# Two of three duos of image 1 take one pair's denominator from scanned sums; the join of the images and the last duo are rearranged

## The chip, the core and the metric

The kernel runs on one core of one Trainium2 chip. Its engines run beside each other and meet by semaphores: TensorE (PE, its weight loads listed as PEld), VectorE (DVE), ScalarE (ACT), GpSimd (POOL), and SyncE (SP), which issues the DMAs. The metric is device microseconds of one execution, lower is better; a kernel's time is the median of its runs. One execution was taken with the hardware profiler, and it has a time and a span of its own.

## What is computed

The input is x, 2 x 128 x 128 x 192 (image, H, W, channel), float32, and the output is x plus a window ratio of the group-normalised x:

```python
def box_sum(x, axis, w): ...        # zero-padded sliding sum of width w
g = _gn(x)                          # 32 groups of 6 channels, mean and variance over H, W and the group
s     = box_sum(g, 2, 5)            # 5 wide along W
num   = box_sum(s * s, 3, 20)       # 20 wide along the channels
d     = box_sum(box_sum(g * g, 2, 5), 3, 20)
denum = d * norm                    # norm: how many columns of W the window really covers
return x + nan_to_num(num / denum, nan=1.0)
```

Mean and variance of an image are needed before any of its centred work can start.

## The kernel before

W lies on the 128 partitions. Four rows of H (768 columns of H and channel) are a duo, made of two pairs of 384 columns; an image has 32 duos, and n runs from 0 to 63 over both images. The load of image 1 and its statistics run beside the duos of image 0. PSUM holds four tiles, S, U, D and N, each of two banks, one bank for a pair; the duo's 384 columns leave 128 columns of each bank spare.

For one duo n of image 1 (and the last ones of image 0) the steps are:

- POOL subtracts the mean, `centre(n)` (line 358, tile xc).
- ACT squares it, `square_xc` (line 422). PE sums both along W with 5-wide bands: `box_u` gives U from the squares, `box_s` gives S from xc (line 520, 128 x 128 blocks).
- ACT copies U to SBUF, `keep_u` (line 436), and squares S, `square_s` (line 446).
- PE sums along the channels with 20-wide bands, scaled by the inverse variance (line 529): `sum_d` gives D, `sum_n` gives N.
- ACT takes the reciprocal root of D and squares it, which gives q (lines 473 and 479).
- DVE runs `quotient(n)`: t1 from D and q (line 776), t2 from N and q (line 779), ratio from both (line 785). A Newton step for the reciprocal is folded into these.
- POOL adds the ratio to x, `finish(n)` (line 364), and SP stores two duos at a time (line 288).

A duo is **summed** if its second pair does not go through `box_u` and `sum_d`. For that pair POOL scales xc to a padded line, `normalise` (line 376), ACT squares the line into the spare half of U, `square_line` (line 428), DVE makes 20-wide sums of it with two scans and an addition, `sum_windows` (lines 746, 749 and 752, result `of_20`), and PE sums `of_20` along W with one wide matmul (line 572). Before, every second duo from 35 on is summed, 15 of them.

The order is written out by hand. On PE each duo n is `sum_d(n)`, `box_u(n+2)`, `sum_n(n)`, `box_s(n+2)`. `sum_d(n)` waits until DVE has read D of duo n-1 (`t1_ready`), `sum_n(n)` until the ratio of n-1 is done (`ratio_ready`), since D and N have one buffer. ACT runs root and square of n, `keep_u(n+2)`, `square_xc(n+3)`, `square_line(n+3)`, `square_s(n+2)`. DVE runs `sum_windows(n+2)` ahead of t1 of n, if n+2 is summed. POOL runs `centre(n+4)`, `normalise(n+4)`, `finish(n)`.

At the **join** of the images, in duo 29, DVE sums the last statistics of image 1 (line 832), PE averages them over the partitions (line 597), DVE copies the mean to SBUF (line 677, in `spread_late`, which also prepares the variance up to line 703), and POOL can centre duo 32, the first of image 1. In duo 30 the variance follows. The **last duo**, 63, ends with an addition on DVE (line 846) in place of POOL's, and a store of its own (line 308).

Of the kernel before, what the change touches and what calls it, by code (L numbers as in the profile page):

```python
# [6 lines left out]
ALU = mybir.AluOpType  # L7
# [4 lines left out]
GROUPS = 32  # L12
# [19 lines left out]
TOTAL = BATCH * DUOS  # L32

# [22 lines left out]
FIRST_SUMMED, SUMMED_EVERY = DUOS + 3, 2  # L56
# [33 lines left out]
def window_ratio_kernel(nc, x, out):  # L90
    ctx = ExitStack()
    with ctx:
# [45 lines left out]
        padded, restart = sums[:, 0:PADDED], sums[:, PADDED:PADDED + LINE]  # L138
        rising, of_20 = sums[:, 1024:1024 + PADDED], sums[:, 1536:1536 + PCOLS]
        scale_c = sums[:, 2048:2048 + PCOLS]  # L140
# [17 lines left out]
        mean_in_psum = sem("mean_in_psum")  # L158
        offsets_in_psum = sem("offsets_in_psum")
# [40 lines left out]
        def d_bank(n):  # L200

            return S if n < SWAPPED and n % 2 else D
# [17 lines left out]
        def summed(n):  # L220
            return FIRST_SUMMED <= n < TOTAL and (n - FIRST_SUMMED) % SUMMED_EVERY == 0

        def nth_summed(n):
            return (n - FIRST_SUMMED) // SUMMED_EVERY
# [47 lines left out]
        def _(sp):  # L272
# [31 lines left out]
            last = TOTAL - 1  # L304
            sp.wait_ge(out_ready, last)
            sp.dma_start(dram_rows(out, last - 1), x_rows(last - 1)).then_inc(stored[1], 16)
# [6 lines left out]
        def _(pool):  # L313
# [53 lines left out]
            def normalise(n):  # L367

                k = nth_summed(n)
                if k:  # L370
                    pool.wait_ge(squares_ready, k)
# [4 lines left out]
                nc.gpsimd.tensor_tensor(rows_of(padded[:, C_LO:PADDED]), pair,  # L376
# [3 lines left out]
            def clear_sums():  # L380

                pool.wait_ge(n_ready, RAW_DUOS)
                nc.gpsimd.memset(padded, 0.0).then_inc(pool_own, 1)
# [9 lines left out]
            for n in range(TOTAL - 1):  # L393
                m = n + CENTRE_AHEAD
                if m == DUOS:
                    for j in range(len(LATE_SETS)):
                        wait_loaded1(pool, j)
                    pool.wait_ge(mean_ready, 2)
                    clear_sums()
# [4 lines left out]
                finish(n)  # L404

        @block.scalar
        def _(act):
# [16 lines left out]
            def square_line(n):  # L424

                act.wait_ge(scaled_ready, nth_summed(n) + 1)
                act.wait_ge(us_ready, n)
                nc.scalar.activation(squares_ps, padded, ACT.Square).then_inc(squares_ready, 1)
# [84 lines left out]
        def _(pe):  # L513
# [37 lines left out]
            def box_u(n):  # L551
# [6 lines left out]
                if summed(n - 1):  # L558
# [302 lines left out]
```

## Time and profile before

| | us |
|---|---|
| median of 3 runs | 382.54 (382.38 to 382.55) |
| the profiled execution, its own time | 381.17 |
| its span | 379.5 |
| PE busy | 355.8 (94%) |
| PE weight loads busy | 349.5 (92%) |
| DVE busy | 298.4 (79%) |
| ACT busy | 273.1 (72%) |
| POOL busy | 249.5 (66%) |
| granted PE clock, mean share of full speed | 0.998 |

Busy shares are means over the whole span and say which engine is nearly full, not which wait ends last at a place; for that the timeline and the chain of waits are read stretch by stretch. Matmul ends are modelled and the matmuls of a block overlap, so a block's length is better read from the chain, where each piece begins as the former ends. A recorded DVE or ACT instruction can end some hundredths of a microsecond after the next one on its engine has started, so what an instruction costs its engine is read from start to start.

### The profile page before, as it was taken

What the parts mean: (1) busy time and instruction counts of PE and PEld (TensorE: products, weight loads), DVE (VectorE), ACT (ScalarE), POOL (GpSimd) and SP (SyncE); (2) the same over time, 40 slices, a digit from 0 to 9 for tenths busy, and PEclk for the clock granted to TensorE, in tenths of its full rate; (3) what the DMA queues carried; (4) which work ended last, traced back from release to release, by engine and by line L of the source; (5) the groups of instructions that cost most, each with busy time, mean ns of one, the idle gap of its engine ahead of it and who ended that gap; (6) DMA issues with size and microseconds to landing.
All of it is one profiled execution on the core that took longest, in us unless ns stands there. A gap on an engine that the chain in (4) does not pass through costs nothing.

```text
span 379.5 us, 7832 instructions
## 1 busy us (share of the span) xinstructions
PE 355.8 (94%) x2960; PEld 349.5 (92%) x2960; DVE 298.4 (79%) x609; ACT 273.1 (72%) x383; POOL 249.5 (66%) x168
## 2 busy tenths in 40 slices
PE   1999979999999999999869999999999999999982
PEld 1999969999999999999869999999999999999981
DVE  2999964766679999999957877777778877777774
ACT  1455559989999999987726777777777777777751
POOL 4000064887888888887158877788777787777631
PEclk9999999999999999999999999999999999999999
DMA  8999300588999973222202222211222222222214
GB/s 243 327 328 329 105 2 0 168 252 263 290 281 282 287 241 106 85 85 83 85 0 85 85 84 85 82 54 53 64 85 85 83 85 85 83 86 83 66 53 134
DMA packets 66486, 50.84 MB, mean 134 GB/s; under 512 B 912, under 2 KB 66448, under 8 KB 66448
## 3 DMA queue, kind: packets, MB, share of 16 engines
q1 hardware_dynamic: 66448, 50.34, 42.8%
q8 instruction: 24, 0.39, 0.4%
q14 instruction: 14, 0.11, 0.1%
HBM read 25.17 MB, written 25.17 MB: 133 GB/s over the span
## 4 chain that ended last, share of the span: by engine, by line
PE 71%; DVE 7%; ACT 5%; issue 2%; POOL 1%; DVEq 0%; POOLq 0%; ACTq 0%
PE N L529 21%; PE U L520 17%; PE D L529 14%; PE S L520 11%; PE S L529 4%; DVE late_triples L668 3%; PE D L572 3%; ACT xs L455 1%; DVE ratio L776 1%; DVE N L779 1%; ACT q L473 1%; ACT xc L422 1%; POOL xc L358 1%; ACT q L479 1%; DVE ratio L785 1%
## 5 line engine op out<-in xcount | busy, mean ns | idle before, releaser
L364 POOL TENSOR_TENSOR xs<-xs,ratio 128x768 f32<-128x768 f32 x63 | 114.6, 1820 | 63.4 <-DVE ratio L785 63.4
L358 POOL TENSOR_TENSOR xc<-xs,mean_c 128x768 f32<-128x768 f32 x64 | 116.9, 1829 | 44.8 <-DVE mean_c L677 44.8
L776 DVE SCALAR_TENSOR_TENSOR ratio<-D,q 128x768 f32<-128x768 f32 x51 | 48.6, 952 | 43.0 <-ACT q L479 43.0
L785 DVE SCALAR_TENSOR_TENSOR ratio<-ratio,N 128x768 f32<-128x768 f32 x64 | 61.1, 954 | 6.4
L779 DVE SCALAR_TENSOR_TENSOR N<-N,q 128x768 f32<-128x768 f32 x64 | 61.5, 960 | 4.9 <-PE N L529 3.1
L473 ACT ACTIVATE q<-D 128x768 f32<-128x768 f32 x51 | 41.4, 811 | 28.1 <-PE D L529 18.4
L479 ACT ACTIVATE q<-q 128x768 f32<-128x768 f32 x64 | 54.1, 846 | 2.0
L520 PE MATMUL S<-b,xc 128*128 128x128 f32 x432 | 54.0, 275 | 0.0
L529 PE MATMUL N<-b_r,xs 128*128 128x138 f32 (+2 forms) x384 | 52.4, 285 | 0.0
L529 PE MATMUL N<-b,xs 128*128 128x138 f32 (+2 forms) x384 | 51.7, 283 | 0.3 <-DVE ratio L785 0.3
L446 ACT ACTIVATE xs<-S 128x768 f32<-128x768 f32 x36 | 29.2, 812 | 31.5 <-PE S L520 31.5
L520 PEld LDWEIGHTS S<-b,xc 128*128 128x128 f32 x432 | 51.2, 191 | 0.0
L529 PEld LDWEIGHTS N<-b,xs 128*128 128x128 f32 x384 | 48.5, 190 | 1.0 <-issue 0.9
L529 PEld LDWEIGHTS N<-b_r,xs 128*128 128x128 f32 x384 | 48.4, 190 | 0.3
L520 PEld LDWEIGHTS U<-b5d,xs 128*128 128x128 f32 x342 | 42.2, 191 | 6.6 <-ACT xs L422 2.9
L520 PE MATMUL U<-b5d,xs 128*128 128x128 f32 x342 | 44.1, 275 | 2.7 <-ACT xs L422 2.7
L668 DVE BATCH_NORM_STATS2 ratio<-xs 128x6 f32<-128x96 f32 x256 | 41.0, 263 | 5.9 <-DMA xs<-x 5.9
L436 ACT ACTIVATE u<-U 128x768 f32<-128x768 f32 (+1 forms) x63 | 45.2, 718 | 0.0
L520 PE MATMUL U<-b5d,xc 128*128 128x128 f32 x336 | 42.3, 276 | 0.8 <-ACT xc L422 0.4
L529 PE MATMUL D<-b,u 128*128 128x137 f32 (+2 forms) x294 | 40.8, 283 | 1.3 <-DVE ratio L776 1.3
L520 PEld LDWEIGHTS U<-b5d,xc 128*128 128x128 f32 x336 | 39.8, 191 | 1.4 <-ACT xc L422 0.9
L529 PEld LDWEIGHTS D<-b,u 128*128 128x128 f32 x294 | 37.6, 190 | 1.4 <-issue 1.4
(89 smaller groups left out, 452.6 us busy)
## 6 DMA issues: line engine op xcount, KB each, us to landing
out<-xs SPq DMA_DIRECT2D x31, 768.0 KB, 3.8
xs<-x SPq DMA_DIRECT2D x8, 1536.0 KB, 14.8
xs<-x SPq DMA_DIRECT2D x16, 768.0 KB, 5.3
out<-xs SPq DMA_DIRECT2D x2, 384.0 KB, 2.6
```

Source lines behind the costliest of these rows:

```text
L358: nc.gpsimd.tensor_tensor(pairs(xc[:, n % XC_RING, :]), pairs(x_flat(n)), mean, ALU.subtract)\
L364: nc.gpsimd.tensor_tensor(x_flat(n), x_flat(n), ratio[:, n % RATIO_RING, :], ALU.add)\
L436: nc.scalar.activation(pairs(u[:, n % U_RING, :])[:, 0:own, :], in_bank(U)[:, 0:own, :], ACT.Copy)\
L446: nc.scalar.activation(pairs(s2_of(n)), in_bank(S), ACT.Square).then_inc(s2_ready, 1)
L473: nc.scalar.activation(pairs(q[:, n % Q_RING, :]), in_bank(d_bank(n)), ACT.Abs_reciprocal_sqrt, bias=-TINY)\
L479: nc.scalar.activation(q[:, n % Q_RING, :], q[:, n % Q_RING, :], ACT.Square).then_inc(q_ready, 1)
L520: mm = nc.tensor.matmul(bank[:, i, chunk], rows[:, at:at + 128], weights[:, :], start=True, stop=True)
L529: mm = nc.tensor.matmul(bank[:, i, first:end], data[:, at:at + 128], b20_r[b][:, SPAN_AT[j]:SPAN_AT[j + 1]], start=j == 0, stop=j == CHUNK ...
L668: return nc.vector.bn_stats(to.rearrange("p g a b -> p (g a b)"), rows)
L776: nc.vector.scalar_tensor_tensor(t1, in_bank(d_bank(n)), -TINY, pairs(q[:, n % Q_RING, :]), ALU.add, ALU.mult).then_inc(t1_ready, 1)
L779: nc.vector.scalar_tensor_tensor(in_bank(N), in_bank(N), TINY, pairs(q[:, n % Q_RING, :]), ALU.add, ALU.mult).then_inc(t2_ready, 1)
L785: nc.vector.scalar_tensor_tensor(t1, t1, 2.0, in_bank(N), ALU.add, ALU.mult).then_inc(ratio_ready, 1)
```

## The change

- Summed duos are now two of three from 35 on: 35, 36, 38, 39, up to 62 and 63, 20 of them. The padded line and `of_20` have two buffers each, the waits between POOL, ACT, DVE and PE follow from that, and `box_u(n)` waits for `of_20` of n-1 only where n is not summed itself. ACT's `square_line` gains a wait for the `of_20` before it.
- At the join, the average of the late means goes to spare columns of U, stands behind `sum_n(29)` on PE and has a semaphore of its own; DVE runs `spread_late` right behind t1 of duo 29, ahead of t2; `box_u(32)` waits until that has ended. POOL finishes duo 28 and clears the buffers before it waits for the mean, and finishes duo 29 after centring 33.
- For the last duo, D goes to S and N goes to U, and its last steps run pair by pair, each pair with its own store.

```diff
-FIRST_SUMMED, SUMMED_EVERY = DUOS + 3, 2
+FIRST_SUMMED, SUMMED_OF = DUOS + 3, (2, 3)
+SUM_RING = 2
...
-        mean_ps = [D[:, 1, 6 * GROUPS:7 * GROUPS], beside[1][:, 0:GROUPS]]
+        mean_ps = [D[:, 1, 6 * GROUPS:7 * GROUPS], U[:, 1, PCOLS:PCOLS + GROUPS]]
...
-            return S if n < SWAPPED and n % 2 else D
+            return S if n < SWAPPED and n % 2 or n == LAST else D
+
+        def n_bank(n):
+
+            return U if n == LAST else N
...
-            return FIRST_SUMMED <= n < TOTAL and (n - FIRST_SUMMED) % SUMMED_EVERY == 0
+            return FIRST_SUMMED <= n < TOTAL and (n - FIRST_SUMMED) % SUMMED_OF[1] < SUMMED_OF[0]
...
-            sp.wait_ge(tail_ready, 1)
-            sp.dma_start(dram_rows(out, last), x_rows(last)).then_inc(stored[0], 16)
-            sp.wait_ge(stored[0], 16 * (BATCH * STEPS // 2 + 1))
+            for i in range(DUO):
+                first = ROWS - DROWS + i * PAIR
+                sp.wait_ge(tail_ready, i + 1)
+                sp.dma_start(out[BATCH - 1, first:first + PAIR, :, :].rearrange("h w c -> w h c"),
+                             x_rows(LAST)[:, i * PAIR:(i + 1) * PAIR, :]).then_inc(stored[0], 16)
+            sp.wait_ge(stored[0], 16 * (BATCH * STEPS // 2 + DUO))
...
                 if m == DUOS:
+                    finish(n)
+                    clear_sums()
                     for j in range(len(LATE_SETS)):
                         wait_loaded1(pool, j)
                     pool.wait_ge(mean_ready, 2)
-                    clear_sums()
                 if m < TOTAL:
                     centre(m)
                 if summed(m):
                     normalise(m)
-                finish(n)
+                if m != DUOS:
+                    finish(n)
...
+                k = nth_summed(n)
+                act.wait_ge(scaled_ready, k + 1)
                 act.wait_ge(us_ready, n)
-                nc.scalar.activation(squares_ps, padded, ACT.Square).then_inc(squares_ready, 1)
+                if k:
+                    act.wait_ge(of_20_ready, k)
+                nc.scalar.activation(squares_ps, padded[k % SUM_RING], ACT.Square).then_inc(squares_ready, 1)
...
-                if summed(n - 1):
+                if n == MEAN_AT + BOX_AHEAD + 1:
+                    pe.wait_ge(ssq_ready, 2)
+                if summed(n - 1) and not summed(n):
                     pe.wait_ge(of_20_ready, nth_summed(n - 1) + 1)
...
+            def finish_last():
+
+                q_of, t1, t2, rows = [pairs(a) for a in (q[:, LAST % Q_RING, :], ratio[:, LAST % RATIO_RING, :])] + [
+                    in_bank(n_bank(LAST)), pairs(x_flat(LAST))]
+                dve.wait_ge(q_ready, LAST + 1)
+                dve.wait_ge(out_ready, LAST - RATIO_RING + 1)
+                nc.vector.scalar_tensor_tensor(t1, in_bank(d_bank(LAST)), -TINY, q_of, ALU.add, ALU.mult)\
+                  .then_inc(t1_ready, 1)
+                dve.wait_ge(n_ready, LAST + 1)
+                nc.vector.scalar_tensor_tensor(t2, t2, TINY, q_of, ALU.add, ALU.mult).then_inc(t2_ready, 1)
+                dve.wait_ge(t1_ready, LAST + 1)
+                dve.wait_ge(t2_ready, LAST + 1)
+                for i in range(DUO):
+                    link(nc.vector.scalar_tensor_tensor(t2[:, i, :], t1[:, i, :], 2.0, t2[:, i, :], ALU.add, ALU.mult))
+                    nc.vector.tensor_tensor(rows[:, i, :], rows[:, i, :], t2[:, i, :], ALU.add).then_inc(tail_ready, 1)
...
-                quotient(n, before_ratio=spread_late if n == MEAN_AT else scale_late_bands if n == VAR_AT else
-                         spread_scale if n == VAR_AT + 1 else None)
+                quotient(n, behind_t1=spread_late if n == MEAN_AT else None,
+                         before_ratio=scale_late_bands if n == VAR_AT else spread_scale if n == VAR_AT + 1 else None)
```

DVE at the join, duo 29, first before and then after the change. The first row is t1; `N<-N,q` is t2, the `mean_c` rows are the copy of the mean, `ssq_c` is the end of the preparation of the variance, and the last row is the ratio.

```order
L776 SCALAR_TENSOR_TENSOR ratio<-D,q 128x768 [waits out_ready,q_ready]
L779 SCALAR_TENSOR_TENSOR N<-N,q 128x2x384 [waits n_ready]
L677 COPY mean_c<-N 128x192 x2
L682 TENSOR_TENSOR late_dev<-late_triples,N 128x128
L682 TENSOR_TENSOR N<-late_triples,N 128x128
L691 TENSOR_TENSOR late_dev<-late_dev,N 128x128 [waits dve_own]
L671 TENSOR_REDUCE N<-late_triples 128x32
L701 TENSOR_REDUCE dev_sum<-late_dev 128x32 [waits dve_own]
L703 SCALAR_TENSOR_TENSOR ssq_c<-dev_sum,N 128x192 [waits dve_own]
L703 SCALAR_TENSOR_TENSOR ssq_c<-dev_sum,N 128x192
L785 SCALAR_TENSOR_TENSOR ratio<-ratio,N 128x768 [waits t2_ready,t1_ready]
```

```order
L807 SCALAR_TENSOR_TENSOR ratio<-D,q 128x768 [waits out_ready,q_ready]
L707 COPY mean_c<-U 128x192 [waits late_mean_in_psum]
L707 COPY mean_c<-U 128x192
L712 TENSOR_TENSOR late_dev<-late_triples,U 128x128
L712 TENSOR_TENSOR N<-late_triples,U 128x128
L722 TENSOR_TENSOR late_dev<-late_dev,N 128x128 [waits dve_own]
L701 TENSOR_REDUCE N<-late_triples 128x32
L732 TENSOR_REDUCE dev_sum<-late_dev 128x32 [waits dve_own]
L734 SCALAR_TENSOR_TENSOR ssq_c<-dev_sum,N 128x192 [waits dve_own]
L734 SCALAR_TENSOR_TENSOR ssq_c<-dev_sum,N 128x192
L812 SCALAR_TENSOR_TENSOR N<-N,q 128x2x384 [waits n_ready]
L818 SCALAR_TENSOR_TENSOR ratio<-ratio,N 128x768 [waits t2_ready,t1_ready]
```

t2, which needs N of duo 29, stood ahead of the copy of the mean and now stands behind all of the preparation.

DVE in image 1. Before, a summed duo's windows (the first three rows) are followed by two duos' t1, t2 and ratio, and then the next windows come:

```order
L746 SCALAR_TENSOR_TENSOR xs<-xs,U 128x400 [waits squares_ready]
L749 SCALAR_TENSOR_TENSOR U<-U,xs 128x394 [waits dve_own]
L752 TENSOR_TENSOR xs<-U,xs 128x384 [waits d_ready,dve_own]
L776 SCALAR_TENSOR_TENSOR ratio<-D,q 128x768 [waits out_ready,q_ready]
L779 SCALAR_TENSOR_TENSOR N<-N,q 128x2x384 [waits n_ready]
L785 SCALAR_TENSOR_TENSOR ratio<-ratio,N 128x768 [waits t2_ready,t1_ready]
L776 SCALAR_TENSOR_TENSOR ratio<-D,q 128x768 [waits out_ready,q_ready]
L779 SCALAR_TENSOR_TENSOR N<-N,q 128x2x384 [waits n_ready]
L785 SCALAR_TENSOR_TENSOR ratio<-ratio,N 128x768 [waits t2_ready,t1_ready]
```

After the change, two such windows have only one duo's t1, t2 and ratio between them:

```order
L777 SCALAR_TENSOR_TENSOR xs<-xs,U 128x400 [waits squares_ready]
L780 SCALAR_TENSOR_TENSOR U<-U,xs 128x394 [waits dve_own]
L783 TENSOR_TENSOR xs<-U,xs 128x384 [waits d_ready,dve_own]
L807 SCALAR_TENSOR_TENSOR ratio<-D,q 128x768 [waits out_ready,q_ready]
L812 SCALAR_TENSOR_TENSOR N<-N,q 128x2x384 [waits n_ready]
L818 SCALAR_TENSOR_TENSOR ratio<-ratio,N 128x768 [waits t2_ready,t1_ready]
L777 SCALAR_TENSOR_TENSOR xs<-xs,U 128x400 [waits squares_ready]
L780 SCALAR_TENSOR_TENSOR U<-U,xs 128x394 [waits dve_own]
L783 TENSOR_TENSOR xs<-U,xs 128x384 [waits d_ready,dve_own]
L807 SCALAR_TENSOR_TENSOR ratio<-D,q 128x768 [waits out_ready,q_ready]
```

Before, windows stood only ahead of the t1 of a summed duo. The second windows of a round now stand ahead of the t1 of a plain duo, and the third t1 of a round has none ahead of it.

PE at the end, D and then N of the last duo, 63. Before:

```order
L529 MATMUL D<-b,u 128x138 [waits t1_ready,us_ready]
L529 MATMUL D<-b,u 128x147
L529 MATMUL D<-b,u 128x137
L572 MATMUL D<-xs,b5d 128x384 [waits of_20_ready]
L529 MATMUL N<-b,xs 128x138 [waits ratio_ready,s2_ready]
```

After:

```order
L551 MATMUL S<-b,u 128x138 [waits s2_ready,us_ready]
L551 MATMUL S<-b,u 128x147
L551 MATMUL S<-b,u 128x137
L599 MATMUL S<-xs,b5d 128x384 [waits of_20_ready]
L551 MATMUL U<-b,xs 128x138 [waits us_ready,s2_ready]
```

D and N of the last duo no longer wait for t1 and the ratio of duo 62, only for steps of ACT.

## Rows read from the trace of the kernel before

**Rows 1.** Busy time by engine, one summed and one plain duo: PE, PEld, DVE, ACT, POOL
```profile
257.51:267.90 10.39, 10.39 (x88) 10.12 (x88) 8.01 (x10) 7.59 (x11) 8.20 (x6) 1.00 0.25 77
```
**Rows 2.** Chain that ended last: start, length, engine, tile, line
```profile
205.97 1.62 PE N L529 x12
...
254.80 1.34 PE S L520 x12
256.14 0.72 PE D L529 x6
256.86 0.65 PE D L572 x2
257.51 0.67 PE U L520 x6
258.18 1.45 PE N L529 x12
...
260.96 1.45 PE D L529 x12
262.41 1.34 PE U L520 x12
```
**Rows 3.** Timeline: start, length, instruction, idle before and what ended it
```profile
255.91 0.95 DVE L785 SCALAR_TENSOR_TENSOR ratio<-ratio,N 128x768 f32<-128x768 f32 x1
...
256.78 0.98 DVE L746 TENSOR_TENSOR_SCAN xs<-xs,U 128x400 f32<-128x400 f32 x1
...
258.82 0.56 DVE L752 TENSOR_TENSOR xs<-U,xs 128x384 f32<-128x384 f32 x1
...
259.29 0.95 DVE L776 SCALAR_TENSOR_TENSOR ratio<-D,q 128x768 f32<-128x768 f32 x1
...
260.15 0.96 DVE L779 SCALAR_TENSOR_TENSOR N<-N,q 128x768 f32<-128x768 f32 x1
...
261.22 0.95 DVE L785 SCALAR_TENSOR_TENSOR ratio<-ratio,N 128x768 f32<-128x768 f32 x1
...
265.23 0.97 DVE L779 SCALAR_TENSOR_TENSOR N<-N,q 128x768 f32<-128x768 f32 x1
```
**Rows 4.** Timeline, N of duo 31 just after the ratio it waits for
```profile
204.82 0.94 DVE L785 SCALAR_TENSOR_TENSOR ratio<-ratio,N 128x768 f32<-128x768 f32 x1
...
205.88 1.51 PEld L529 LDWEIGHTS N<-b_r,xs 128*128 128x128 f32 x12
```
**Rows 5.** Timeline, the join of the two images
```profile
190.33 0.95 DVE L776 SCALAR_TENSOR_TENSOR ratio<-D,q 128x768 f32<-128x768 f32 x1
...
190.56 0.38 PE L597 MATMUL N<-mean_sum,averager 128*128 128x32 f32 x2 [1.94 <-DVE mean_sum L832]
...
193.38 0.61 DVE L677 COPY mean_c<-N 128x192 f32<-128x192 f32 x2
...
194.20 0.45 POOL L383 MEMSET xs<- 128x424 f32 x1 [11.03 <-DVE mean_c L677]
...
195.17 1.81 POOL L358 TENSOR_TENSOR xc<-xs,mean_c 128x768 f32<-128x768 f32 x1
195.25 0.62 DVE L703 SCALAR_TENSOR_TENSOR ssq_c<-dev_sum,N 128x192 f32<-128x192 f32 x2
...
197.91 1.60 PE L520 MATMUL U<-b5d,xs 128*128 128x128 f32 x12 [2.66 <-ACT xs L422]
```
**Rows 6.** Chain that ended last, from D of duo 62 to the end
```profile
364.87 1.46 PE D L529 x12
...
369.18 0.96 PE D L529 x6
...
375.47 0.96 DVE xs L846
```
**Rows 7.** DMA issues: queue, count, size each, us from issue to landing
```profile
out<-xs SPq DMA_DIRECT2D x31, 768.0 KB, 3.8
...
out<-xs SPq DMA_DIRECT2D x2, 384.0 KB, 2.6
```

More of the change, by code:

```diff
@@ L137, in window_ratio_kernel @@
         sums = xs[:, SUM_SLOT * STEP:(SUM_SLOT + 2) * STEP, :].rearrange("p r c -> p (r c)")
-        padded, restart = sums[:, 0:PADDED], sums[:, PADDED:PADDED + LINE]
-        rising, of_20 = sums[:, 1024:1024 + PADDED], sums[:, 1536:1536 + PCOLS]
-        scale_c = sums[:, 2048:2048 + PCOLS]
+        sizes = (PADDED, PADDED, LINE, PADDED, PCOLS, PCOLS, PCOLS)
+        ends = [sum(sizes[:i]) for i in range(len(sizes) + 1)]
+        padded_0, padded_1, restart, rising, of_20_0, of_20_1, scale_c = [
+            sums[:, a:b] for a, b in zip(ends, ends[1:])]
+        padded, of_20 = (padded_0, padded_1), (of_20_0, of_20_1)
         rows_of = lambda line: line[:, 0:PAIR * PITCH].rearrange("p (r c) -> p r c", r=PAIR)[:, :, 0:C]
@@ L220, in summed, with nth_duo @@
         def summed(n):
-            return FIRST_SUMMED <= n < TOTAL and (n - FIRST_SUMMED) % SUMMED_EVERY == 0
+            return FIRST_SUMMED <= n < TOTAL and (n - FIRST_SUMMED) % SUMMED_OF[1] < SUMMED_OF[0]
         def nth_summed(n):
-            return (n - FIRST_SUMMED) // SUMMED_EVERY
+            rounds, rest = divmod(n - FIRST_SUMMED, SUMMED_OF[1])
+            return rounds * SUMMED_OF[0] + rest
+        def nth_duo(k):
+            return FIRST_SUMMED + k // SUMMED_OF[0] * SUMMED_OF[1] + k % SUMMED_OF[0]
         def own_pairs(n):
@@ L303, in _ @@
                 store(t)
-            last = TOTAL - 1
-            sp.wait_ge(out_ready, last)
-            sp.dma_start(dram_rows(out, last - 1), x_rows(last - 1)).then_inc(stored[1], 16)
-            sp.wait_ge(tail_ready, 1)
-            sp.dma_start(dram_rows(out, last), x_rows(last)).then_inc(stored[0], 16)
-            sp.wait_ge(stored[0], 16 * (BATCH * STEPS // 2 + 1))
+            sp.wait_ge(out_ready, LAST)
+            sp.dma_start(dram_rows(out, LAST - 1), x_rows(LAST - 1)).then_inc(stored[1], 16)
+            for i in range(DUO):
[4 more added lines that the diff above has]
+            sp.wait_ge(stored[0], 16 * (BATCH * STEPS // 2 + DUO))
             sp.wait_ge(stored[1], 16 * (BATCH * STEPS // 2))
@@ L382, in clear_sums @@
                 pool.wait_ge(n_ready, RAW_DUOS)
-                nc.gpsimd.memset(padded, 0.0).then_inc(pool_own, 1)
+                nc.gpsimd.memset(sums[:, 0:SUM_RING * PADDED], 0.0).then_inc(pool_own, 1)
                 nc.gpsimd.memset(restart, 1.0).then_inc(pool_own, 1)
@@ L564, in sum_d @@
                 pe.wait_ge(us_ready, n + 1)
-                if d_prev(n) >= 0:
+                if n == LAST:
+                    pe.wait_ge(s2_ready, n + 1)
+                elif d_prev(n) >= 0:
                     pe.wait_ge(t1_ready, d_prev(n) + 1)
@@ L570, in sum_d @@
                 if summed(n):
-                    pe.wait_ge(of_20_ready, nth_summed(n) + 1)
-                    mm = nc.tensor.matmul(D[:, 1, 0:PCOLS], b5d[:, :], of_20, start=True, stop=True)
+                    k = nth_summed(n)
+                    pe.wait_ge(of_20_ready, k + 1)
+                    mm = nc.tensor.matmul(d_bank(n)[:, 1, 0:PCOLS], b5d[:, :], of_20[k % SUM_RING], start=True, stop=True)
                 mm.then_inc(d_ready, 1)
@@ L577, in sum_n @@
                 pe.wait_ge(s2_ready, n + 1)
-                if n:
+                if n == LAST:
+                    pe.wait_ge(us_ready, n + 1)
+                elif n:
                     pe.wait_ge(ratio_ready, n)
@@ L842, in _ @@
                     unmeasured.remove((j, g))
-            n = TOTAL - 1
-            quotient(n)
-            dve.wait_ge(ratio_ready, n + 1)
-            nc.vector.tensor_tensor(x_flat(n), x_flat(n), ratio[:, n % RATIO_RING, :], ALU.add).then_inc(tail_ready, 1)
+            finish_last()
 def kernel(x):
```

27 lines of the change are left out of this document (16 added, 11 removed).

## The prediction

> **What bounds the kernel now.** I read three views, in this order. First the busy time of a stretch of image 1 that holds one summed and one plain duo [rows 1]: of 10.39 us PE is busy in all 10.39, with the granted clock at 1.00, while DVE is busy for 8.01, ACT for 7.59 and POOL for 8.20. So PE sets the pace there, and a duo is worth what it keeps PE busy. Second the chain that ended last [rows 2]: it runs through PE alone, block after block, and gives each block's price. Third the timeline at the two places where PE does wait: the join [rows 5], where it waits 1.94 us for the sum of the statistics and 2.66 us for the first square of image 1, and the end [rows 6], where the work of one duo hangs step behind step.
>
> The sum is made against the profiled execution, 381.17 us with a span of 379.5, and the saving is then taken off the median, 382.54.
>
> **Five more summed duos.** A plain duo is N 1.45, S 1.34, D 1.45, U 1.34: 5.58 us of PE. A summed one has D 0.72 + 0.65 and U 0.67, so 4.83 [rows 2]. The two make 10.41, and rows 1 show 10.39. Each further summed duo saves 0.67 of U and 0.08 of D, 0.75. Twenty in place of fifteen are five; up to the start of D of duo 62 all of U and four of the D parts are gone, 5 x 0.67 + 4 x 0.08 = **-3.67 us** on the path.
>
> What the others take on: a plain duo costs DVE three steps of 0.95, of which start to start 0.86 + 1.07 + 0.87 = 2.80, and windows 2.04 + 0.47 = 2.51 [rows 3]. A round of three duos is then 3 x 2.80 + 2 x 2.51 = 13.42 us of DVE against 5.58 + 2 x 4.83 = 15.24 of PE. For POOL a summed duo is what rows 1 leave beside a plain duo's centre and finish of 1.81 each [rows 5], 8.20 - 3.62 = 4.58, so a round is 12.8; for ACT even two whole pairs of duos would be 2 x 7.59 = 15.18. So no engine becomes the bound by its load. Order is another matter, since D and N have one buffer.
>
> **The tightest leg.** Take duos 53 and 54, summed, 55, plain, and 56, summed, and let N of 53 end at 0. No windows stand ahead of t1 of 53, so its t2 waits for that N alone. PE goes on with S 1.34, D 1.37, U 0.67, N 1.45, S 1.34, D 1.45, U 0.67, N 1.45, S 1.34 and wants to begin D of 56 at 11.08. Its loads run ahead: in rows 4 the loads of N began at 205.88 and the block ended at 205.97 + 1.62 = 207.59 [rows 2], so they began 1.71 before the end of a block of 1.45, 0.26 ahead. The release is therefore wanted at 11.08 - 0.26 = 10.82. On DVE t2 starts at 0.03 (262.41 + 1.34 + 1.45 = 265.20, t2 at 265.23), the ratio at 1.10, the windows of 56 at 1.97, the addition at 4.01, t1 of 54 at 4.48. Its q is no earlier: D of 54 ends at 2.71, and t1 follows a D by 259.29 - 257.51 = 1.78 at the soonest, so 4.49. Then t2 at 5.35, the ratio at 6.42, the windows of 57 at 7.29, the addition at 9.33, t1 of 55 at 9.80, ended at 10.75 [rows 3]. PE's loads begin 205.88 - (204.82 + 0.94) = 0.12 behind such an end [rows 4], at 10.87. That is 0.05 late. A late release costs PE about its lateness: in rows 4 the loads were some 0.17 behind (205.88 for a wanted 205.97 - 0.26), and the block took 1.62 in place of 1.45. There are nine such legs, to D of 38, 41 and so on up to 62, so 9 x 0.05 = **+0.45 us**. The bounds of a leg are 0 (an earlier release by 0.05) and 0.47, worked out below.
>
> The other new waits: ACT's square_line now waits for the addition before it, and square_s of the same step is queued behind it on ACT, for which PE's next S and N wait. In the leg the addition ends at 4.57, and ACT reaches square_line no sooner than q of 54 (4.49) plus two short copies, near 5.1. So it costs nothing, with 0.5 us in hand. POOL's longer order (centre, normalise, finish in two duos running) is worked four duos ahead and has 2.4 us of room in a round. Both ring buffers only loosen waits. `box_u` of a summed duo loses its wait for `of_20` and gains none.
>
> **The join.** Before, DVE made t1 at 190.33, waited for N and copied the mean at 193.38; POOL then cleared its buffers from 194.20 and centred duo 32 at 195.17; after ACT's square, U began at 197.91 [rows 5]. Now the average on PE can still not begin before 190.56, and ends at 190.94, its new tile being free by then. DVE is free 0.87 after the start of t1, at 191.20, and copies the mean there, 2.18 sooner. POOL has cleared its buffers while it waited (it sat idle 11.03 us), so the 195.17 - 194.20 = 0.97 of clearing leave the path as well: **-3.15 us** for centre, square and U of 32, which now begins at 194.76. What is late next: `spread_late` takes 195.25 + 0.62 - 193.38 = 2.49 and ends at 193.69, so the new wait of `box_u(32)` for it lies 1.07 under cover; were that cover gone it would be paid one for one. t2 and the ratio of duo 29 follow at 193.7 and 194.8, and the next N needs them at 194.76 + 1.34 and more. On PE S of 31 and D of 30 follow the average, 190.94 + 1.34 + 1.45 = 193.73, ahead of U. The longer memset (848 for 424 columns, at most double 0.45) and the moved finish of 28 lie in POOL's idle time; finish of 29 goes behind one more centre of 1.81, while its ratio comes late anyway. Low bound of the saving: 2.18, if the clearing is hidden already by something that I don't see. I take 3.15, as each piece of it is on the chain.
>
> **The last duo.** From the start of D of 62 to the end of the last addition it is 376.43 - 364.87 = 11.56 [rows 6]. Now, from the start T: D of 62 (summed) ends at T + 1.37, its t1 is at T + 3.15. N of 62 waits for the ratio of 61: t1 of 61 is the 9.80 of the leg above, where D of 62 starts at 11.08 or T, so it started at T - 1.28, t2 at T - 0.42, the ratio at T + 0.65, ended at 1.60, and N begins to be loaded at 1.72. N ends 1.71 behind the start of its loads, as above, at T + 3.43; before, D of 63 also had its wait and 0.96 for 0.72 behind it [rows 2, 6]. Now D of 63 follows at once in its new tile to 4.80, t1 at T + 6.58, t2 at 7.44. Then the two halves: a step on 384 columns is 0.56 [rows 3], and with 0.08 for its link and 0.10 saved where the next may overlap, ratio 8.51, sum 9.15, ratio 9.61, sum 10.25 to 10.81. So 10.81 for 11.56: **-0.75 us**. The halves themselves cost 0.35, and the tiles gain 1.1.
>
> The last store is 192 KB for 384. Stores of 768 and 384 KB take 3.8 and 2.6 us [rows 7]; half the step again gives 2.0, **-0.6 us**, with 0 as the other bound, since three stores now land within 5 us.
>
> By the Trainium skill (DMA: Bandwidth & Descriptors, Anatomy of one DMA) a DMA is some 2.0 us fixed and its bytes over 436 GB/s. That would save 0.45, and the sum would be 0.15 smaller; rows 7 have the steeper slope.
>
> **Sum.** -3.67 + 0.45 - 3.15 - 0.75 - 0.6 = -7.7 us: span 371.8, the profiled execution 373.5, median 382.54 - 7.7 = **374.8 us**.
>
> **Rivals.**
>
> A. DVE's leg is later than 0.05, and the rounds go by DVE. For it: the leg is tight to a twentieth of a microsecond, and it hangs on DVE starting before the former record ends (t2 starts 0.86 after a t1 of 0.95). If each waited for the end of the one ahead, six steps would come 0.08 to 0.09 later, and t1 would reach PE at about 11.29, 0.47 late; 9 x 0.47 = 4.2 in place of 0.45 gives 378.6 us. Against: the starts in rows 3 show the overlap in each of these pairs. It decides from 0.05.
>
> The Trainium skill (VectorE: DVE Perf Modes, Terms) says of the pipeline flush after every DVE operation that the next "can't issue until 8-slice pipe empties". Taken by the records that would be this rival and 378.6; the trace disagrees as far as starts go, 0.86 for 0.95.
>
> B. The join gives its time to another wait. The centre of 32 is ready 3.15 sooner, but U of 32 waits for the end of `spread_late`, since the mean lies in its bank. If those steps are stretched beyond 1.07, or PE's average is held by ACT's copy of U of 31, the gain shrinks; at none of it the time is 378.0. Against: nothing in rows 5 waits for that copy, and PE's idle time ahead of the average is put down to the sum alone.
>
> C. Slower than before: windows ahead of t1 for both kinds of duo. The two scans and the addition are the only thing between a plain duo's ratio and its t1, and two buffers of the line do nothing for the one buffer of D. To lose the gain of 7.7, each of nine legs must be late by 0.05 + 0.86, so the four scans of a leg must take 1.2 us each for 0.98. Then 382.6 and above; at 1.3 each 385. For it: scans in U run while PE writes U's other bank more often than before. Against: in rows 1 PE is busy throughout, so the scans of rows 3 already run beside its matmuls.
>
> D. The change does not save on PE, because the square line or `of_20` comes last for D of a summed duo. In the leg `of_20` of 57 is there at 9.89, and PE comes to the matmul that reads it at 11.08 + 1.37 + 1.34 + 1.45 + 1.34 + 0.72 = 17.3, so it has 0.02.
>
> **How the numbers follow.** The forecast has 0.68, for 373.8 to 375.7: its low end is the leg at 0 and the tail 0.5 better, its high end the DMA term at 0 and some more of the leg. A has 0.18, 375.7 to 379; B 0.07, 375.7 to 378; C 0.03; D 0.02 and what I don't see 0.02, both counted as slower. The range is 373.8 to 377.3, which leaves out the far half of A, parts of B, and C. A measurement of this kernel can tell 0.2%, 0.8 us, from no change. Faster by more: 0.94; within: 0.01; slower: 0.05.
>
> **What would show it.** In the trace after: D of every duo n behind a plain one (38, 41, ...) either follows S at once or shows PE waiting for t1; PE busy share near 1 over the rounds and 15.2 us for three duos. At the join, centre of 32 near 192.0 and U near 194.8, with idle time of PE of 0.6 and 1.0. At the end 10.8 us from D of 62 to the last addition, and 2.0 for the last store. I am wrong if the round takes 15.7 or more, or if U of 32 starts behind 195.5.

## The result

| | before | after |
|---|---|---|
| median, us | 382.55 (382.38 to 382.74, 4 runs) | 373.4 (373.3 to 373.56, 4 runs) |
| profiled execution, its own time | 381.17 | 373.3 |
| its span | 379.5 | 371.6 |

The ratio is 0.9761, with a 95% interval of 0.9744 to 0.9778. The change saves 9.15 us where 7.7 were forecast, and 373.4 lies below the range, which began at 373.8. Between the two profiled executions the saving is 7.87, and the span forecast for the changed kernel, 371.8, is 0.2 from the one measured. So the sum held on the profile, and the error lies in how it was carried to the median.

The page of the changed kernel has the engines' busy time, the busy tenths of PE and the granted clock in 40 slices of the span:

```profile
PE 353.1 (95%) x2910; PEld 345.7 (93%) x2910; DVE 309.3 (83%) x626; ACT 271.6 (73%) x388; POOL 254.8 (69%) x173
...
PE   1999989999999999999989999999999999999992
...
PEclk9999999999999999999999999999999999999998
```

PE is busy for 353.1 us in place of 355.8, DVE for 309.3 in place of 298.4, and one 8 is left where the join was 8 and 6.

**The join.** The timeline of the changed kernel there (start, length, instruction, idle time ahead and what ended it) answers to [rows 5]:

```profile
188.59 0.81 POOL L400 MEMSET xs<- 128x848 f32 x1
...
190.25 0.95 DVE L807 SCALAR_TENSOR_TENSOR ratio<-D,q 128x768 f32<-128x768 f32 x1
...
190.48 0.38 PE L625 MATMUL U<-mean_sum,averager 128*128 128x32 f32 x2 [0.49 <-DVE mean_sum L881]
...
191.12 0.61 DVE L707 COPY mean_c<-U 128x192 f32<-128x192 f32 x2
...
191.95 3.59 POOL L375 TENSOR_TENSOR xc<-xs,mean_c 128x768 f32<-128x768 f32 x2 [1.98 <-issue]
...
193.00 0.62 DVE L734 SCALAR_TENSOR_TENSOR ssq_c<-dev_sum,N 128x192 f32<-128x192 f32 x2
...
194.70 1.60 PE L542 MATMUL U<-b5d,xs 128*128 128x128 f32 x12 [0.96 <-ACT xs L441]
```

The mean is copied at 191.12 (forecast 191.20), centred at 191.95 (192.0), U begins at 194.70 (194.76). PE's idle times there are 0.49 and 0.96 us, where they were 1.94 and 2.66. N of duo 29 now fills most of the first.

**The rounds.** N of duo 31, D of duo 35 and then one round of three duos on the chain of waits (start, length, blocks), to be read beside [rows 2]:

```profile
202.76 1.45 PE N L551 x12
...
220.92 0.78 PE D L551 x6
...
226.46 0.72 PE D L551 x6
227.19 0.65 PE D L599 x2
227.83 0.67 PE U L542 x6
228.50 1.45 PE N L551 x12
229.94 1.34 PE S L542 x12
231.28 1.45 PE D L551 x12
232.73 0.67 PE U L542 x6
233.40 1.45 PE N L551 x12
234.84 1.34 PE S L542 x12
236.18 0.79 PE D L551 x6
236.97 0.65 PE D L599 x2
```

All of the round is PE, end to end, and the D behind the second windows takes 0.79 for 0.72. That is the tight leg, late by 0.07 where 0.05 was forecast. D of duo 35 is late too, with 0.78: the windows of 35 and of 36 both stand ahead of it, so the kernel has ten such legs up to D of 62, where the prediction counted nine. The next D of this kind stands at 251.46, so a round takes 251.46 - 236.18 = 15.28 us (forecast 15.2). N of duo 31 took 1.62 before, as the ratio it waits for came late [rows 4], and takes 1.45 now: 0.17 that the join gives on top, and that the prediction had in its rows but not in its sum.

**The end.** The timeline of the changed kernel, beside [rows 6], and the issues of the stores, beside [rows 7]:

```profile
358.23 0.79 PEld L551 LDWEIGHTS D<-b,u 128*128 128x128 f32 x6
...
360.19 1.68 PE L551 MATMUL N<-b,xs 128*128 128x138 f32 x12 [0.33 <-DVE ratio L818]
...
365.00 0.96 DVE L826 SCALAR_TENSOR_TENSOR ratio<-S,q 128x768 f32<-128x768 f32 x1 [0.48 <-ACT q L501]
...
368.59 0.56 DVE L834 TENSOR_TENSOR xs<-xs,U 128x384 f32<-128x384 f32 x1
```

```profile
out<-xs SPq DMA_DIRECT2D x1, 384.0 KB, 2.6
out<-xs SPq DMA_DIRECT2D x2, 192.0 KB, 2.0
```

With the loads of D of duo 62 begun at 358.23, the block counts from 0.26 later, 358.49; the last addition ends at 369.15, 10.66 behind it (forecast 10.81, before 11.56). The span ends 2.45 later, before it was 3.07.

### The profile page after: what moved, and what is told of

Read it like the earlier page. It is cut to its first block, busy times and chain, and to the rows that moved or that the text cites. A ratio compares the mean times of both kernels' runs of the same rounds, so it can differ in the third digit from the quotient of the medians.

```text
span 371.6 us, 7774 instructions
## 1 busy us (share of the span) xinstructions
PE 353.1 (95%) x2910; PEld 345.7 (93%) x2910; DVE 309.3 (83%) x626; ACT 271.6 (73%) x388; POOL 254.8 (69%) x173
## 4 chain that ended last, share of the span: by engine, by line
PE 69%; DVE 9%; ACT 6%; issue 2%; POOL 1%; DVEq 0%; POOLq 0%; ACTq 0%
PE N L551 21%; PE U L542 16%; PE D L551 13%; PE S L542 11%; PE S L551 4%; PE D L599 3%; DVE late_triples L698 3%; ACT xs L477 1%; DVE ratio L807 1%; DVE N L812 1%; ACT q L495 1%; ACT xc L441 1%; POOL xc L375 1%; DVE ratio L818 1%; ACT q L501 1%
## 5 line engine op out<-in xcount | busy, mean ns | idle before, releaser
L807 DVE SCALAR_TENSOR_TENSOR ratio<-D,q 128x768 f32<-128x768 f32 x50 | 47.5, 950 | 25.5 <-ACT q L501 25.5
L818 DVE SCALAR_TENSOR_TENSOR ratio<-ratio,N 128x768 f32<-128x768 f32 x63 | 60.1, 954 | 6.4
L812 DVE SCALAR_TENSOR_TENSOR N<-N,q 128x768 f32<-128x768 f32 x63 | 60.4, 959 | 3.3 <-PE N L551 1.8
L551 PE MATMUL N<-b,xs 128*128 128x138 f32 x372 | 50.0, 283 | 0.3 <-DVE ratio L818 0.3
L551 PEld LDWEIGHTS N<-b,xs 128*128 128x128 f32 x372 | 47.0, 190 | 0.9 <-ACT xs L468 0.9
L542 PEld LDWEIGHTS U<-b5d,xs 128*128 128x128 f32 x312 | 39.1, 191 | 6.0 <-ACT xs L441 1.2
L458 ACT ACTIVATE u<-U 128x768 f32<-128x768 f32 (+1 forms) x63 | 43.5, 691 | 0.0
L542 PE MATMUL U<-b5d,xs 128*128 128x128 f32 x312 | 40.7, 275 | 1.0 <-ACT xs L441 1.0
L551 PE MATMUL D<-b,u 128*128 128x137 f32 (+2 forms) x258 | 36.9, 286 | 0.0
L551 PEld LDWEIGHTS D<-b,u 128*128 128x128 f32 x258 | 33.2, 190 | 0.0
## 6 DMA issues: line engine op xcount, KB each, us to landing
out<-xs SPq DMA_DIRECT2D x2, 192.0 KB, 2.0
```

What stands on the lines that cost most here:

```text
L458: nc.scalar.activation(pairs(u[:, n % U_RING, :])[:, 0:own, :], in_bank(U)[:, 0:own, :], ACT.Copy)\
L542: mm = nc.tensor.matmul(bank[:, i, chunk], rows[:, at:at + 128], weights[:, :], start=True, stop=True)
L551: mm = nc.tensor.matmul(bank[:, i, first:end], data[:, at:at + 128], b20_r[b][:, SPAN_AT[j]:SPAN_AT[j + 1]], start=j == 0, stop=j == CHUNK ...
L807: nc.vector.scalar_tensor_tensor(t1, in_bank(d_bank(n)), -TINY, pairs(q[:, n % Q_RING, :]), ALU.add, ALU.mult).then_inc(t1_ready, 1)
L812: nc.vector.scalar_tensor_tensor(in_bank(N), in_bank(N), TINY, pairs(q[:, n % Q_RING, :]), ALU.add, ALU.mult).then_inc(t2_ready, 1)
L818: nc.vector.scalar_tensor_tensor(t1, t1, 2.0, in_bank(N), ALU.add, ALU.mult).then_inc(ratio_ready, 1)
```

## The experiments

Each was timed beside the kernel before on the same chip: 1 to 4, 5 to 8 and 9 to 12 on three chips. Differences to the changed kernel are taken to the 373.42 of experiment 2, from 5 on thus across chips; the runs of before with a mean clock of 0.997 or 0.998 have 381.26, 381.33 and 381.22 as their middle ones there, so that costs some 0.1. A run's own mean granted PE clock is recorded with its time, and the runs are sorted by it. It is a rough sorting, since the mean also has the time behind the last matmul: from 370 to 371 us in the profile of the changed kernel PE has nothing to do and the granted clock is 0.50. Eight of this kernel's nine runs took 373.2 to 373.6, with mean clocks of 0.994 to 0.997.

**1. The kernel before once more.** No edit.

> The kernel before, unchanged, timed and profiled once more. The profiled execution of before took 381.17 us where its ordinary runs took 382.4 to 382.7, and the changed kernel shows no such gap (373.3 and 373.4). Theory 1: single executions of this kernel have two lengths some 1.3 us apart, and the profile caught the short one; then the runs here are mostly 382.5, and this profile has 382.5 with a stretch in it that is 1.3 us longer than in the first profile. Theory 2: the profiled execution is always shorter for this kernel, so the profile has 381.2 again beside runs of 382.5. Theory 3: the chip of the first profile differed, and here both agree.

Twelve runs took 381.24 to 386.1 us, median 382.74. The 23 runs of before beside them took 381.12 to 384.45, median 382.26. This profile's execution took 382.23, with a span of 380.5. The busy time by stretch (PE, PEld, DVE, ACT, POOL, then the granted clock) has the missing microsecond. First the stretch from 191 to 195 us of the first profile of before, then of this one:

```profile
191.00:195.00 4.00, 4.00 (x36) 4.00 (x35) 2.74 (x9) 0.00 (x0) 0.80 (x2) 1.00 0.00 0
```

```profile
191.00:195.00 4.00, 4.00 (x22) 4.00 (x22) 1.70 (x5) 0.00 (x0) 0.00 (x0) 0.57 0.00 0
```

PE is busy in both, but with 22 matmuls for 36: the granted clock is 0.57 in place of 1.00, and from 192 to 194 it is 0.50, the lower of its two levels (1.2 for 2.4 GHz). The timeline shows what came before and what it delays:

```profile
190.51 0.38 PE L597 MATMUL N<-mean_sum,averager 128*128 128x32 f32 x2 [1.93 <-DVE mean_sum L832]
190.72 2.77 PE L529 MATMUL N<-b_r,xs 128*128 128x138 f32 x12
...
193.53 0.97 DVE L779 SCALAR_TENSOR_TENSOR N<-N,q 128x768 f32<-128x768 f32 x1 [2.30 <-PE N L529]
194.40 0.61 DVE L677 COPY mean_c<-N 128x192 f32<-128x192 f32 x2
...
198.93 1.60 PE L520 MATMUL U<-b5d,xs 128*128 128x128 f32 x12 [2.08 <-ACT xs L422]
```

PE had been idle for 1.93 us. Then N of duo 29 took 2.77 for 1.69, t2 waited 2.30 us for it, and the copy of the mean, which before the change stands behind t2, came at 194.40 in place of 193.38. U of duo 32 follows 1.02 later than in [rows 5], and the span is 1.0 longer. PE's wait ahead of that U is 0.58 shorter than in [rows 5], 2.08 for 2.66, and takes up the rest of the lost time. So theory 1 holds, except that there are more than two lengths.

Over all experiments the kernel before ran 69 times. In 17 runs the mean clock was 0.997 or 0.998, and these took 381.11 to 381.58, middle one 381.26. The other 52 had 0.984 to 0.994 and took 381.35 to 386.1. Nineteen of them, with 0.992 to 0.994, took 382.23 to 382.86 as this profile's execution did (0.993), and the four runs of the result's table, 382.38 to 382.74, lie there too. The other groups are 0.990 and 0.991 (13 runs, 381.35 to 382.21), 0.985 and 0.986 (9 runs, 382.83 to 383.4), 0.988 (8 runs, 384.17 to 384.69) and 0.984 (3 runs, 385.38 to 386.1); no profile of this kernel was taken in one of them.

**2. The changed kernel once more.** No edit.

> The changed kernel, unchanged, beside the same runs of before. Theory 1: 373.4 us in the runs, ratio 0.976; the profile within 0.2 of them, or 1.3 longer or shorter if this kernel has two lengths too. Theory 2: the profile 373.3. The gain in us between profiles that both are long or both short would be 7.9.

373.42 us (373.22 to 374.45, 5 runs), ratio 0.9771 (0.9742 to 0.98); the profiled execution took 373.46. The changed kernel has one length, with one run of five, of the lowest mean clock (0.993), a microsecond above it.

**3. The join undone.** Main edits:

```diff
-        mean_ps = [D[:, 1, 6 * GROUPS:7 * GROUPS], U[:, 1, PCOLS:PCOLS + GROUPS]]
+        mean_ps = [D[:, 1, 6 * GROUPS:7 * GROUPS], beside[1][:, 0:GROUPS]]
...
+                if n == MEAN_AT:
+                    average_late_means()
                 if n == VAR_AT:
                     average_squares(1)
                 box20(n_bank(n), s2_of(n), batch(n)).then_inc(n_ready, 1)
...
-                quotient(n, behind_t1=spread_late if n == MEAN_AT else None,
-                         before_ratio=scale_late_bands if n == VAR_AT else spread_scale if n == VAR_AT + 1 else None)
+                quotient(n, before_ratio=spread_late if n == MEAN_AT else scale_late_bands if n == VAR_AT else
+                         spread_scale if n == VAR_AT + 1 else None)
```

> The changed kernel with the order of before at the join alone (mean of image 1 in N's bank, average ahead of N of duo 29, mean copied behind t2, buffers cleared and duo 28 finished as before). By the terms of my sum 3.15 us longer than the changed kernel: 376.55. If the missing 1.4 us sit at the join, 377.9.

378.56 us (377.13 to 381.76, 12 runs), 2.0 above the sum of terms, and the spread of before is back. Its profile has 1.92 us of idle time ahead of the average, and behind it:

```profile
191.00:195.00 4.00, 4.00 (x23) 4.00 (x23) 1.42 (x4) 0.00 (x0) 0.00 (x0) 0.60 0.00 0
```

The missing time does sit at the join, though it is no fixed 1.4 us. The second idle time is 2.71 us in this profile, and the clock behind it stays at 1.00.

**4. The last duo undone.** Main edits (the last duo's banks and steps as before):

```diff
-            return S if n < SWAPPED and n % 2 or n == LAST else D
+            return S if n < SWAPPED and n % 2 else D
...
-            finish_last()
+            n = TOTAL - 1
+            quotient(n)
+            dve.wait_ge(ratio_ready, n + 1)
+            nc.vector.tensor_tensor(x_flat(n), x_flat(n), ratio[:, n % RATIO_RING, :], ALU.add).then_inc(tail_ready, 1)
```

> The changed kernel with the last duo of before (D and N of duo 63 in their usual banks, one ratio and one addition on DVE, one store of 384 KB). By the terms of my sum 0.75 + 0.6 = 1.35 us longer: 374.75. If the missing 1.4 us sit at the end, 376.1.

374.8 us (374.7 to 375.92, 5 runs): +1.4, as the terms had it. The execution that was profiled is the one of 375.92, and it shows that the join is not the only place. In it PE was idle for 1.87 us near 49 us, ahead of the mean of image 0, and from 50 to 52 us:

```profile
50.00:52.00 2.00, 2.00 (x10) 2.00 (x10) 1.57 (x5) 0.00 (x0) 0.54 (x1) 0.50 0.00 0
```

That idle time ends with DVE's statistics, which wait for the loads. It is 0.68 and 1.38 us in the two profiles of the changed kernel and 2.47 in that of experiment 5, where the clock behind it stays at 1.00; the change leaves this place as it is.

**5. The first idle time of the old join filled.** The kernel before with one line more, in `sum_n`:

```diff
                 if n == MEAN_AT:
+                    box20(N, s2_of(n), batch(n))
                     average_late_means()
```

> The kernel before with N of duo 29 summed twice: once ahead of PE's average of the late means, where PE sat idle 1.93 us, and once in its place (the second overwrites the first with the same sums). Idle time there falls to about 0.5 us and nothing else moves. Clock theory: in the second profile of before the granted clock was 0.57 from 191 to 195 us, behind that idle time, and the execution was 1.06 us longer than the first profile's, whose clock was 1.00 there. With the gap filled the clock stays at 1.00 there and the median falls from about 382.4 to 381.2, with less spread. Rival: the spread of before comes from elsewhere (loads, the end), and the median stays at 382.4.

384.45 us (381.19 to 385.77, 12 runs). Two runs took 381.2, as expected, and ten took 384.4 to 385.8. The first idle time is 0.40 now and the clock behind it 1.00. But the second is still 2.65:

```profile
198.05 2.07 PE L520 MATMUL U<-b5d,xs 128*128 128x128 f32 x12 [2.65 <-ACT xs L422]
```

```profile
199.00:203.00 4.00, 4.00 (x20) 4.00 (x20) 0.96 (x1) 2.67 (x4) 4.00 (x3) 0.50 0.02 4
...
204.00:205.00 1.00, 1.00 (x6) 1.00 (x6) 0.32 (x1) 0.00 (x0) 0.21 (x1) 0.50 1.01 325
```

Behind it the clock is 0.50 from 199.0 to about 205.7, some 7 us, about twice as long as in experiment 1 (191.2 to 194.5). Half of that is lost, and the chain shows no later wait of PE that would take it up, so it costs 3.2 us in place of 1. My expectation had overlooked the second place; the median moved the wrong way, and yet by the same cause.

**6. The idle time made in the changed kernel.**

```diff
+                if n == MEAN_AT:
+                    pe.wait_ge(mean_sum_ready, 1)
                 if n == VAR_AT:
                     average_squares(1)
```

> The changed kernel with PE waiting for the sum of the late statistics ahead of N of duo 29, not behind it, so that PE is idle for 1.9 us ahead of it as before the change. The average and the mean come 1.45 us later: 373.4 + 1.45 = 374.85 if the clock stays. Clock theory: in most executions the clock is halved for some 3 us behind the gap, N takes 2.6 to 2.9 for 1.45, and the median is 375.9 to 376.2, with a spread of 1 to 2 us. Rival: 374.85 with the spread of the changed kernel, 0.2.

375.37 us (374.74 to 376.63, 6 runs). Two runs, with mean clocks of 0.997 and 0.998, took 374.74 and 374.76, the 374.85 of the undisturbed case; three took 375.3 to 375.5 and one 376.63, with 0.985 to 0.990. The profile of one of these:

```profile
190.66 2.06 PE L551 MATMUL N<-b_r,xs 128*128 128x138 f32 x12 [1.93 <-DVE mean_sum L883]
...
192.81 2.74 PE L542 MATMUL S<-b,xc 128*128 128x128 f32 x12
```

So idle time of 1.9 us brings the slow stretch and the spread to the changed kernel as well. Its price was expected at 1.2 and is 0.6 to 0.8 in most runs: part of it falls on S and D of the join, and the idle time of 0.96 that PE had behind them, ahead of U of 32, is gone from this profile.

**7. Every second duo summed.** `SUMMED_OF = DUOS + 3, (1, 2)` in the changed kernel.

> The changed kernel with every second duo summed, as before the change (15 duos; join, last duo and the two buffers as changed). My terms: 3.67 on PE's path, less 0.45 for the tight leg, so 3.2 us longer than the changed kernel, 376.6; if DVE's leg costs nothing, 377.1. The legs show in the profile as D blocks of 0.79 for 0.72 in the changed kernel and should be gone here.

376.11 us (375.8 to 376.22, 6 runs), +2.7 for 3.2 expected. The profile splits it. All D blocks of summed duos are 0.72 again. D of duo 62 starts at 361.76; U of 32 was 0.26 later than in the other profile, so 361.76 - 0.26 - 358.49 = 3.0 lie ahead of it. The term is 3.67 less the ten legs of 0.07, 2.97. From there to the last addition it is 10.31 in place of 10.66, since ahead of t1 of 61 stands one duo's windows and not two in a row, and N of 62 need not wait for the ratio of 61: a saving of the old pattern that I had not counted.

**8. DVE a little longer.**

```diff
                                         rows_of(rising), ALU.add).then_inc(of_20_ready, 1)
+                nc.vector.memset(sums[:, 2880:3008], 0.0)
```

> The changed kernel with one more instruction on DVE behind each sum_windows, a memset of 128 unused columns, some 0.15 to 0.2 us. If DVE's two windows and their t1 are the tight leg (late by 0.07 in the profile), each of the nine rounds gets two of these in its leg: 9 x 2 x 0.17 = 3.1 us, 376.5. If PE alone sets the pace and DVE has the room that its busy share suggests (13.2 of 15.3 us), nothing: 373.4.

375.14 us (374.81 to 375.33, 5 runs), +1.7. The leg is DVE's, as the same D on the chain shows:

```profile
236.51 0.96 PE D L551 x6
```

It takes 0.96 for 0.79, 0.17 a round, nine times 1.5 us, and D of 35 0.89 for 0.78. I had expected 0.34 a round. The memset puts t1 off by 0.14, since it overlaps its neighbours, t2 then starts 0.05 nearer to t1, and the last t1 of the leg is itself 0.05 shorter (0.90). So DVE, at 83% busy, has no room at all in this leg.

**9. Both idle times of the old join shortened.** The kernel before with the line of experiment 5, and S of duo 31 summed again behind D of duo 30, its signal given by the second:

```diff
                 sum_d(n)
+                if n == MEAN_AT + 1:
+                    box5(S, xc_of(n + 1), b5).then_inc(s_ready, 1)
```

> The kernel before with both idle times of PE at the join shortened by repeated work: N of duo 29 is summed twice, and S of duo 31 is summed again behind D of duo 30. With the first alone filled, ten of twelve runs took 384.4 to 385.8 and two 381.2; their profile has the clock at 0.50 behind the second idle time, 2.65 us, from 198 on. Clock theory: with gaps of 0.4 and 1.3 us no clock drop follows, and nearly all runs take 381.2 to 381.5, as the runs of before do that have a mean clock of 0.998. Rival: the repeated work itself costs, or drops come anywhere; the median stays above 382.

381.1 us (380.91 to 382.43, 12 runs), beside 382.0 for before: ratio 0.9985 (0.9972 to 0.9998). Ten of the twelve runs took 380.91 to 381.27; the other two, 382.25 and 382.43, have a mean clock of 0.991. The timeline shows both idle times shortened:

```profile
190.33 0.41 PE L600 MATMUL N<-mean_sum,averager 128*128 128x32 f32 x2 [0.40 <-DVE mean_sum L837]
...
197.71 1.60 PE L520 MATMUL U<-b5d,xs 128*128 128x128 f32 x12 [1.33 <-ACT xs L422]
```

Two blocks of twelve matmuls, whose sums are thrown away, make the kernel before about a microsecond faster at the median. That is the missing term by itself, as far as it sits at the join.

**10. The old join in the changed kernel, filled.** Experiment 3 with the two lines of 5 and 9.

> The changed kernel with the join undone, as timed before (378.56), and the same two fillings. Without clock drops the join's own term is left: 373.4 + 3.15 = 376.55, all runs within some 0.4. The 2.0 us between this and 378.56 would be what the clock takes from the old join in this kernel. If the join's term is larger than I worked out, it stays above 377.

376.97 us (376.85 to 377.03, 4 runs). The spread of experiment 3 (377.13 to 381.76) is gone, and its median falls by 1.6. What is left to the changed kernel, 376.97 - 373.42 = 3.55, is the join's own worth. I had 3.15. One part of the difference is the clearing, which with two buffers is longer and in this order stands on the path:

```profile
194.04 0.80 POOL L400 MEMSET xs<- 128x848 f32 x1 [10.97 <-DVE mean_c L707]
```

U of 32 starts at 198.10, 3.40 behind the changed kernel's 194.70, and N of duo 31 takes 1.63 for 1.45 as it did in the kernel before; the two give 3.58.

**11. One store at the end.** The changed kernel with SP waiting for both halves and one DMA of 384 KB.

> The changed kernel with one store of 384 KB for the last duo behind both halves, in place of two of 192 KB. By the issue rows (2.6 and 2.0 us to landing) 0.6 us longer, 374.0; if the stores ahead of it set the end, 373.4.

373.89 us (373.8 to 374.27, 5 runs), +0.5. In the profile the span ends 3.05 behind the last addition, for 2.45 with two stores: 0.60.

**12. Three of four duos summed.** `SUMMED_OF = DUOS + 3, (3, 4)` in the changed kernel.

> The changed kernel with three of four duos summed, 22 of them. PE has 2 x 0.75 us less to do, and DVE's load of 4 x 2.80 + 3 x 2.51 = 18.7 us still fits into PE's 5.58 + 3 x 4.83 = 20.1 for four duos: by loads alone 371.9 to 372.4. By the leg: a summed duo with windows ahead of its t1 takes DVE 5.31 us and PE 4.83, so a third one in a row makes the leg later by 0.48, to some 0.55, seven times, 3.8 us, while nine times 0.07 fall away: 373.4 - 1.5 + 3.8 - 0.6 = 375.1.

375.82 us (374.59 to 376.37, 4 runs). The profiled execution, 376.37, has a clock of 0.72 from 50 to 56 us, behind 1.89 us of idle time there. The run of 374.59 has the highest mean clock, 0.997, and stands for the undisturbed kernel: 1.2 above the changed one. The profile has the same 1.2, if one takes off that its U of 32 starts at 196.50, 1.80 later. That is nearer to the 375.1 of the leg than to the 372 of the loads; 0.35 of what is missing lies at the end, where D of 62 to the last addition takes 10.31 as in experiment 7. The chain of waits now runs through DVE for long stretches:

```profile
242.03 0.95 DVE ratio L807
242.98 0.88 DVE N L812
243.96 0.95 DVE ratio L818
244.91 0.91 DVE xs L777
245.85 1.00 DVE U L780
246.90 0.44 issue
247.34 0.96 DVE ratio L807
```

From t1 (the first row) to t1 (the last) with one duo's windows between it is 247.34 - 242.03 = 5.31 us, where PE needs 4.83. Of the three patterns tried, two of three is the best.

## Why the prediction was right and where it failed

| term | forecast | measured |
|---|---|---|
| join | -3.15 | -3.21 between the profiles' U of 32 (197.91 and 194.70), and -0.17 in N of 31 |
| five summed duos | -3.67 | -3.70: D of 62 at 358.49 for 364.87, -6.38, without the join's 3.38 and the leg's 0.70 |
| the tight leg | +0.45 | +0.70 (ten legs, late by 0.07 each) |
| last duo | -0.75 | -0.90 |
| last store | -0.6 | -0.62 in the profiles, 0.5 by experiment 11 |
| sum | -7.7 | -7.9 in the span |

The steps of the sum held within 0.25 us each, and the span came out within 0.2 partly by luck: the leg cost 0.25 more than forecast, the join with N of 31 gave 0.23 more and the last duo 0.15 more. The two terms worked out from waits alone are confirmed as waits by experiments that move little else: the leg by 8 and 12, the join by 10. Of rival A the leg was late by 0.07 and not by 0.47 (its sum has five pairs of neighbours and not the six that it names); what its rule asks, that an operation waits for the end of the one ahead, is not what DVE does, as two neighbours on the changed kernel's timeline show, t2 0.87 behind the start of a t1 of 0.95:

```profile
229.61 0.95 DVE L807 SCALAR_TENSOR_TENSOR ratio<-D,q 128x768 f32<-128x768 f32 x1
230.48 0.96 DVE L812 SCALAR_TENSOR_TENSOR N<-N,q 128x768 f32<-128x768 f32 x1
```

Rival B did not come: `spread_late` ended at 193.62, 1.1 ahead of U. Rival C needed scans of 1.2 us, and they kept their 0.98. Rival D did not come either: in the round above the part of D that reads `of_20` (line 599) takes its 0.65 with no wait. By the Trainium skill (DMA: Bandwidth & Descriptors, Anatomy of one DMA) a DMA is some 2.0 us fixed and its bytes over 436 GB/s, which as an estimate makes 0.45 of the smaller store and 2.45 of the landing of 192 KB. The page gives this for DMAs issued on GpSimd, and these stores are issued on SyncE. The trace does not agree with it: the landing is 2.0 in the rows above, on the slope of [rows 7], and the profile of experiment 11 has 0.60 between one store and two; its median, 0.47, cannot tell 0.45 from 0.6.

The step that failed is the first one of the sum: "the saving is then taken off the median, 382.54". The profiled execution of before took 381.17, 1.37 less than its ordinary runs. I carried that difference over as if it belonged to every kernel. It belongs to the old join: in the second profile of before, which took 382.23 as the runs of the table did, the granted clock fell to its lower level behind 1.93 us of idle PE, and N, for which the mean of image 1 waited, took 2.8 for 1.7 us. The first profile caught an execution without it, like 17 of the 69 in the experiments. So the profile of before that I read was of a kernel 1.3 us better than its median, and the change removes the idle time as a side effect of putting N into it. From the undisturbed 381.26 the forecast would have been 373.6, against 373.4 measured. So of the 9.15 us that the change saves at the median, some 7.9 are the terms of the sum and some 1.3 are the clock at the old join, which the prediction had at nothing.

Shown are: that the clock falls behind idle times of 1.87 to 2.65 us of PE (six profiles: experiments 1, 3, 4, 5, 6 and 12), that at the join it did not fall behind idle times of 0.96 (experiments 2, 7 and 8), 1.33 (9) and 1.67 us (10), that with the gaps shortened the median of before falls to 381.1, and that a gap put into the changed kernel brings the loss back. Not shown is why an idle time of 1.93 us is followed by a fall in one run and not in the next. Its length alone does not decide: the first profile had both idle times of the old join and a clock of 1.00, and no fall came behind 2.08 us in experiment 1, 2.47 in experiment 5 and 2.71 in experiment 3. Nor is it shown where the runs of before outside the group of the second profile lost their time. The eight with 0.988 and 384.17 to 384.69 are like the profile of experiment 5 (0.987, 384.43), with a fall behind the second idle time; the thirteen with 0.990 and 0.991 may have theirs near 49 us, where the profiles of experiments 4 and 12, variants of the changed kernel, have it. Both are guesses from the mean clock.

The sign of trouble was in the table of times: runs within 0.2 us of each other, and a profiled execution 1.2 under the lowest of them. A rival of the kind "the ordinary runs lose time that this execution did not" was worth a chance of its own, with the two idle times of [rows 5] as the place.

## What to carry to other kernels

Compare the profiled execution's time with the median before using its rows: where they differ by more than the runs do among themselves, the profile is of another case than the one that is timed, and the difference is a term of the sum to be placed, not a constant to be carried over. A wait of PE costs its length and, in some runs, a slow stretch behind it; work that stands behind the wait but does not need it is best put ahead, even where nothing seems to wait for it. And an engine at 80% busy can have no room at all, if two of its longer jobs stand in a row ahead of the one that another engine needs: read the leg start to start before counting on its idle share.

## What the runs showed of the hardware that I had not expected

- Idle times of PE as short as 1.87 and 1.93 us are followed by some 3 us or more at the lower clock level, in some executions of a program and not in others: 52 of 69 runs of the kernel before have a mean clock under 0.997, and idle times of 2.47 and 2.71 us had no fall behind them in two profiles. In the profile of experiment 5 the clock is at 0.50 from 199 to 205 us, behind 2.65 us of idle time.
- The price depends on how long the slow stretch is and on what stands behind. Blocks ahead of a wait absorb part of it (0.6 us left in experiment 6, 1.0 in experiment 1, each with some 3 us at the lower level), and some 7 us at the lower level in a stretch in which PE itself sets the pace cost 3.2 (experiment 5).
- Doing a block of matmuls twice can make a kernel faster, 381.1 for 382.0 us in experiment 9.
- A slightly late release costs PE about its lateness and no more: D of 0.79 for 0.72, where 0.05 late was worked out, and 0.96 where experiment 8 puts DVE's t1 off by 0.17 more.
